# The sort's column sweep: loops written out, and VectorE making the scaled one-hots of three columns in five instead of two

## The reference

```python
def _gat_layer(x, src, dst, W, b, a, g, beta, N, concat):
    h = x @ W.T + b
    score = (h @ a[:d])[src] + (h @ a[d:])[dst]
    e = jnp.exp(-jax.nn.leaky_relu(score, ALPHA))
    h_prime = jax.ops.segment_sum(e[:, None] * h[dst], src, num_segments=N)
    ...                       # layer norm, elu
x = x + gnn(layernorm(x), ..., edge_index=[src, dst])   # 8 heads, then one output layer
x = x + moe(layernorm(x), ...)                          # 8 experts, the best 2
```

## Time and profile before

| what | value |
|---|---|
| median of three runs | 5569.01 us |
| profiled execution | 5574.75 us, of it 5573.0 us from its first to its last instruction |
| the sweep on VectorE | from 338.12 us (first L743) to 1096.45 us (last L738) |
| busy in the whole span | PE 84%, DVE 77%, POOL 73%, ACT 39% |
| mean granted clock of TensorE | 0.945 |

### The profile page before, as it was taken

One profiled execution on the slowest core, in us unless ns is written; L12 is line 12 of the kernel. 1 busy time (PEld: TensorE's weight loads), 2 busy tenths in 40 slices (PEclk: granted clock), 3 DMA queues, 4 the chain that ended last, 5 costly groups with the idle time before them and its releaser, 6 DMA issues. The chain is left out here.

```text
span 5573.0 us, 94092 instructions
## 1 busy us (share of the span) xinstructions
PE 4664.7 (84%) x20462; PEld 2641.7 (47%) x20462; DVE 4308.8 (77%) x15028; ACT 2185.1 (39%) x5836; POOL 4043.8 (73%) x4498
## 2 busy tenths in 40 slices
PE   7888888878888888888888866888788888888888
PEld 4532222333333333333333334666666666666666
DVE  6679999978888888888888866666666666666665
ACT  2258888723433344334333430222222222222223
POOL 2269999757777777777777757777777777777773
PEclk9999999989999999999999987999999999999999
DMA  3200000068888888888888865555555555554551
GB/s 76 66 17 1 0 0 0 1 191 246 242 243 242 243 243 243 244 243 243 242 243 242 242 184 158 137 137 140 137 138 140 137 139 138 137 140 136 139 141 53
DMA packets 331594, 847.59 MB, mean 152 GB/s; under 512 B 75165, under 2 KB 105167, under 8 KB 331187
## 3 DMA queue, kind: packets, MB, share of 16 engines
q0 software_dynamic: 219136, 683.92, 43.0%
q1 hardware_dynamic: 109763, 158.20, 9.7%
q10 hardware_dynamic: 2288, 0.79, 0.1%
HBM read 816.28 MB, written 26.36 MB: 151 GB/s over the span
## 5 line engine op out<-in xcount | busy, mean ns | idle before, releaser
L1382 POOL DMA_INDIRECT out_rows<-table,shared_node_of x1712 | 1641.8, 959 | 558.6 <-issue 479.5
L1137 POOL DMA_INDIRECT heads_rows<-table,shared_node_of x1712 | 1621.5, 947 | 575.0 <-issue 536.3
L1311 PE MATMUL heads_banks<-heads_rows,heads_hot 128*128 128x512 f32 x3424 | 1743.9, 631 | 140.1 <-DVE heads_rows L1193 136.0
L1527 PE MATMUL out_banks<-out_rows,out_hot 128*128 128x256 f32 x3424 | 1105.5, 416 | 121.9 <-DVE out_hot L1421 119.3
L1193 DVE TENSOR_TENSOR heads_rows<-heads_rows,heads_ps_k 128x512 f32<-128x512 f32 x1712 | 1163.0, 680 | 1.0
L1259 ACT ACTIVATE sums<-heads_banks x856 | 511.8, 598 | 1295.1 <-PE heads_banks L1311 1294.7
L1311 PEld LDWEIGHTS heads_banks<-heads_rows,heads_hot 128*128 128x128 f32 x3424 | 575.4, 193 | 674.8 <-DVE heads_rows L1193 327.4
L1527 PEld LDWEIGHTS out_banks<-out_rows,out_hot 128*128 128x128 f32 x3424 | 678.0, 206 | 311.5 <-DVE out_hot L1421 192.2
L582 POOL TENSOR_SCALAR sort_plain_lane<-sort_lanes_h,sort_place 125x128 f16<-125x128 f16 x990 | 688.8, 707 | 78.7 <-ACT sort_by_lane L893 62.7
L2064 PE MATMUL moe_ps_y<-late_w,moe_hidden 128*125 128x256 f32 x1600 | 536.6, 425 | 212.1 <-DVE moe_result L1957 153.7
L1487 ACT ACTIVATE out_weight<-out_score 128x4 f32<-128x4 f32 x428 | 87.8, 205 | 1415.8 <-DVE out_score L1416 1414.9
(11 more groups left out here) (347 smaller groups left out, 5847.6 us busy)
## 6 DMA issues: line engine op xcount, KB each, us to landing
heads_lanes<-lane_rows SPq DMA_DIRECT2D x214, 256.0 KB
out_lanes<-lane_rows SPq DMA_DIRECT2D x214, 256.0 KB
heads_rows<-table,shared_node_of POOLq DMA_INDIRECT x1712
out_rows<-table,shared_node_of POOLq DMA_INDIRECT x1712
table<-proj_rows SPq DMA_DIRECT2D x50, 227.5 KB
table<-mid_rows SPq DMA_DIRECT2D x50, 113.8 KB
sort_member<-in_x SPq DMA_DIRECT2D x5, 1120.0 KB
moe_x_raw<-in_x SPq DMA_DIRECT2D x50, 112.0 KB
```

The costliest lines, as they stand in the source:

```text
L1137: nc.gpsimd.indirect_dma_start(out=rows[:, g % RING, j, :], out_offset=None, in_=table[:, :], in_offset=bass.IndirectOffsetOnAxis(ap=node_ ...
L1311: ins = nc.tensor.matmul(banks[:, bass.ds(info[r], width)], hot[:, g % HOTS, j, :], rows[:, g % RING, j, 0:width], start=False, stop=True, ...
L1382: nc.gpsimd.indirect_dma_start(out=rows[:, g % RING, j, :], out_offset=None, in_=table[:, :], in_offset=bass.IndirectOffsetOnAxis(ap=node_ ...
L1527: ins = nc.tensor.matmul(banks[:, g % BANKS, j // RUN, :], hot[:, g % HOTS, j, :], rows[:, g % RING, j, 0:FEAT], start=j % RUN == 0, stop= ...
```

## The change

`SCALED` becomes (1, 3): slots 0, 2 and 4 are made by VectorE, so a turn has eleven VectorE instructions, six of them lane one-hots, and GpSimd and ScalarE make the lanes of two columns. The three hardware loops of VectorE, ScalarE and TensorE are written out column by column, with fixed places and fixed wait values; `hold` and its semaphore go, ScalarE's two waits stand directly ahead of the activation. The number of scaled columns ahead of column n is worked out by `scaled_before`.

```diff
-def hold(eng, sem, value, scratch):
-
-    eng.wait_ge(sem, value)
-    eng.sem_inc(scratch, 1)
...
-        SCALED = (1, 3, 4)
-        PER_TURN, SCALED_PART = COLUMNS // SLOTS * len(SCALED), PCOLS // SLOTS * len(SCALED)
+        SCALED = (1, 3)
         LANES_AHEAD = 5
+        def scaled_before(n):
+
+            return n // SLOTS * len(SCALED) + sum(at < n % SLOTS for at in SCALED)
...
-                for n in range(PCOLS):
+                for n in range(part * PCOLS, (part + 1) * PCOLS):
                     if n % SLOTS in SCALED:
+                        made = scaled_before(n)
                         if made >= LANES_AHEAD:
                             pool.wait_ge(s["scaled"], made - LANES_AHEAD + 1)
...
-                with dve.Fori(0, PCOLS // COLUMNS) as i:
-                    for j in range(COLUMNS):
-                        n = i * COLUMNS + j
-                        slot = j % SLOTS
-                        value_at = bass.ds(n + part * PCOLS, 1)
+                for n in range(part * PCOLS, (part + 1) * PCOLS):
+                    slot, value_at = n % SLOTS, slice(n, n + 1)
+
+                    dve.wait_ge(s["slot_used"], n + 1)
+                    if slot not in SCALED:
+                        nc.vector.tensor_scalar(by_lane[:, slot, 0, :], lanes_h[:, :], lane[:, value_at], low[:, value_at],
+                                                ALU.is_equal, ALU.mult)
+                        nc.vector.tensor_scalar(by_lane[:, slot, 1, :], lanes_h[:, :], lane[:, value_at], high[:, value_at],
+                                                ALU.is_equal, ALU.mult)
+                    nc.vector.tensor_scalar(by_tile[:, slot, :], count_tiles_h[:, :], tile[:, value_at], None, ALU.is_equal)\
+                        .then_inc(s["slot_made"], 1)
...
-                with act.Fori(first, last) as i:
-                    for j in range(COLUMNS):
-                        if j % SLOTS in SCALED:
-                            here, slot = SCALED.index(j % SLOTS), j % SLOTS
-                            n = j // SLOTS * len(SCALED) + here
-                            hold(act, s["lane_made"], i * PER_TURN + (part * SCALED_PART + n + 1), s["held_act"])
-                            hold(act, s["slot_used"], i * COLUMNS + (part * PCOLS + j + 1), s["held_act"])
+                for n in range(part * PCOLS + first * COLUMNS, part * PCOLS + last * COLUMNS):
+                    slot, value_at = n % SLOTS, slice(n, n + 1)
+                    if slot in SCALED:
+                        made = scaled_before(n)
+                        act.wait_ge(s["lane_made"], made + 1)
+                        act.wait_ge(s["slot_used"], n + 1)
...
-                with pe.Fori(first, last) as i:
+                for n in range(part * PCOLS + first * COLUMNS, part * PCOLS + last * COLUMNS):
+                    slot = n % SLOTS
+                    pe.wait_ge(s["slot_made"], n + 1)
+                    if slot in SCALED:
+                        pe.wait_ge(s["scaled"], scaled_before(n) + 1)
```

More of the change, by code:

```diff
@@ L511, in sort_edges @@
                  "numbered lane_made scaled slot_made slot_used swept packed_made packed_turned turn_out reach_made step_made "
-                 "step_known route_made route_used block_known row_ready laid_out dst_used cast held_act lane_known is_keyed is_spread is_compared picked "
+                 "step_known route_made route_used block_known row_ready laid_out dst_used cast lane_known is_keyed is_spread is_compared picked "
                  "local_made local_turned lane_kept lanes_stored")
@@ L577, in _ @@
                     pool.wait_ge(s["lane_known"], 1)
-                for n in range(PCOLS):
+                for n in range(part * PCOLS, (part + 1) * PCOLS):
                     if n % SLOTS in SCALED:
+                        made = scaled_before(n)
                         if made >= LANES_AHEAD:
                             pool.wait_ge(s["scaled"], made - LANES_AHEAD + 1)
-                        nc.gpsimd.tensor_scalar(plain_lane[:, made % LANES_AHEAD, :], lanes_h[:, :], lane[:, part * PCOLS + n:part * PCOLS + n + 1], None,
-                                                ALU.is_equal).then_inc(s["lane_made"], 1)
-                        made += 1
+                        nc.gpsimd.tensor_scalar(plain_lane[:, made % LANES_AHEAD, :], lanes_h[:, :], lane[:, n:n + 1], None, ALU.is_equal)\
+                            .then_inc(s["lane_made"], 1)
         @block.vector
@@ L882, in scale_columns @@
             def scale_columns(part, first, last):
-                with act.Fori(first, last) as i:
-                    for j in range(COLUMNS):
-                        if j % SLOTS in SCALED:
-                            here, slot = SCALED.index(j % SLOTS), j % SLOTS
-                            n = j // SLOTS * len(SCALED) + here
-                            hold(act, s["lane_made"], i * PER_TURN + (part * SCALED_PART + n + 1), s["held_act"])
-                            hold(act, s["slot_used"], i * COLUMNS + (part * PCOLS + j + 1), s["held_act"])
[L891 to L894, removed]
+                for n in range(part * PCOLS + first * COLUMNS, part * PCOLS + last * COLUMNS):
[4 more added lines that the diff above has]
+                        act.wait_ge(s["slot_used"], n + 1)
+                        nc.scalar.activation(by_lane[:, slot, 0, :], plain_lane[:, made % LANES_AHEAD, :], ACT.Copy, scale=low[:, value_at])
+                        nc.scalar.activation(by_lane[:, slot, 1, :], plain_lane[:, made % LANES_AHEAD, :], ACT.Copy,
+                                             scale=high[:, value_at]).then_inc(s["scaled"], 1)
             def take_sums(part):
@@ L995, in sweep_columns @@
             def sweep_columns(part, first, last):
-                with pe.Fori(first, last) as i:
[L998 to L1007, removed]
+                for n in range(part * PCOLS + first * COLUMNS, part * PCOLS + last * COLUMNS):
[3 more added lines that the diff above has]
+                        pe.wait_ge(s["scaled"], scaled_before(n) + 1)
+                    for number, ps in enumerate((ps_a, ps_b)):
+                        ins = nc.tensor.matmul(ps[:, part % 2, 0:PART_TILES], by_lane[:, slot, number, :], by_tile[:, slot, :],
+                                               start=False, stop=False)
+                    ins.then_inc(s["slot_used"], 1)
             def turn_sums(part):
```

10 lines of the change are left out of this document (removed).

## The result

The changed kernel takes 5686.99 us (median of four runs, 5683.77 to 5688.82), the kernel before 5568.78 us (median of four): a ratio of 1.0197, 95% interval 1.0172 to 1.0222, or +118 us. The prediction was 5690 us, in a range of 5660 to 5745.

What follows compares the result with a forecast made beforehand. VectorE was taken to bound the sweep: own work 812.8, borders 3.9, waits 8.8 and hold-up 53.4 give 878.9 us against 758.3, +120.6. On the median of 5569.01 that gave 5690 us, range 5660 to 5745.

Steps and rivals of the forecast that it cites:

- What bounds the sweep: In the sweep, VectorE sets the pace: busy 125.00 of 125 us, with the other engines' wait chains ending at it.
- Clean pitches, 0.223 and 0.225 us: VectorE in the sweep after GpSimd's last lane: 0.223 us per lane instruction, 0.225 per L757, start to start.
- Part one: Three columns in five on VectorE: 660 more lane instructions, +147.2 us; 330 fewer GpSimd lanes, -26.7 us of hold-up.
- part three: Start of the sweep: extra lane instructions lie in VectorE's wait for TensorE, so the start stays at 8.8 us.
- Part two: Sweep loops written out: ending the register work costed at nothing; bounds 0 to a few us, or a gain.
- The hold-up, 0.081 us per GpSimd lane: VectorE's remainder of 80.0 us in the sweep before, over 990 GpSimd lanes; 53.4 us for the new 660.
- the sum of 878.9 us: Forecast sweep on VectorE: own work 812.8, borders 3.9, waits 8.8, hold-up 53.4 us; against 758.3 before.
- The bounds of 0.05 and 0.16: Hold-up in us per GpSimd lane in common and long turns of the sweep; +100 to +173 us for the change.
- Lane instructions that become shorter when written out: Rival in the sweep: loop register work is the lane pitch, which falls toward 0.141 us; -42 us, 5527; chance 0.04.
- No hold-up: Rival in the sweep: GpSimd's hold-up of VectorE mostly goes; sweep 825.5 us, +67, 5636 us; chance 0.09.
- TensorE at half clock: Rival in the sweep: matmuls 0.31 us apart make TensorE the bound, 3.06 us per turn; +264, 5833 us; chance 0.03.
- GpSimd's lane as a full stop of VectorE: Rival in the sweep: each of 660 lanes stops VectorE some 0.6 us; +463, 6032 us; chance 0.02.

Runs made afterwards that it cites:

- e3_no_gpsimd: Changed kernel with SCALED empty, so VectorE makes the lanes of all five columns; +351 us against the kernel before, ratio 1.0554.
- e7_act_written: Kernel before with SCALED (1, 3) and ScalarE's loop alone written out; +124 us against the kernel before, ratio 1.0196.
- e2_ratio_only: Kernel before with SCALED (1, 3) alone, hardware loops kept; +145 us against the kernel before, ratio 1.0225.
- e10_by_tensor: e1_written_out with GpSimd waiting for TensorE's slot_used in place of ScalarE's scaled; -35 us against the kernel before, ratio 0.9929.
- e12_lane_later: Changed kernel with GpSimd also waiting for VectorE's tile of fifteen columns back; +149 us against the kernel before, ratio 1.0262.
- e1_written_out: Changed kernel with SCALED back at (1, 3, 4), loops still written out; -12 us against the kernel before, ratio 0.9979.
- e9_by_vector: e1_written_out with GpSimd also waiting for VectorE's tile ten columns back; +2 us against the kernel before, ratio 1.0001.
- e4_lanes_beside: e3_no_gpsimd plus 660 unused GpSimd lanes for slots 1 and 3; +388 us against the kernel before, ratio 1.0606.
- e8_block_of_three: Changed kernel with SCALED (2, 3, 4) in place of (1, 3); +51 us against the kernel before, ratio 1.0082.
- e11_memset_beside: e4_lanes_beside with GpSimd's unused comparisons replaced by memsets; +367 us against the kernel before, ratio 1.0650.

## Why the prediction was right, and where by luck

**What bounds the sweep**: right. VectorE was busy through it, and TensorE waited for its tiles; the sum of pitches alone gave the two sweeps without comparisons on GpSimd, 1114.0 and 1116.5 us, to 1.3 us. In the others the hold-up is what this sum leaves over, so they don't test it.

**Clean pitches, 0.223 and 0.225 us**: right to 1.2 us in 1114 (`e3_no_gpsimd`). They had been read from the last 3 us of the sweep, where GpSimd has ended, and not from the mean durations of 0.32 and 0.34.

**Part one, 660 more lane instructions, +147.2 us**: right. `e3_no_gpsimd` has 1320 more still, and its sweep is 1114.0 where the sum had 1120; most of the difference is in the waits at the start, 4.2 us and not 8.8. VectorE's longer head start takes 1.1 us off its first wait, and the second wait, 2.9 us in the kernel before, isn't there when no lane comes by way of ScalarE. In the changed kernel the two were 4.6 and 2.6, together 7.2: part three, which kept the start at 8.8, was 1.6 us off.

**Part two, the loops at nothing**: wrong in this term. The register work of VectorE is free, as the prediction had it (`e7_act_written`, 3 us in the time and none in the sweep), and so are its 66 jumps back, for which the prediction had left room for a gain. But "ScalarE and TensorE wait for VectorE anyway" looked only for their own time. ScalarE's delay moves GpSimd's lanes, and VectorE pays for where they start. At the new ratio the loop of ScalarE costs 31 us of sweep (905.9 against 874.5), at the old one the three loops together cost 13.0 (758.3 against 745.3); which of them, no run took apart.

**The hold-up, 0.081 us per GpSimd lane**: a good figure for the wrong reason. I took the mean over the turns of before as a price; it is no price but a place. The new ratio alone raises it to 0.122 (`e2_ratio_only`, +145 us, beyond the +120.6 of the sum but inside the +100 to +173), and the written-out loop brings it down to 0.074. Two errors nearly cancel: with the loops the hold-up was 80.3 us and not 53.4 (26.9 more), and writing them out took 31.5 off again (80.3 to 48.8). That they do is luck. What remains between the sum of 878.9 us and the measured 872.7 is 4.6 us of hold-up and 1.6 of waits. The bounds of 0.05 and 0.16 from the two kinds of turns held all kernels with a comparison on GpSimd, 0.053 to 0.124, and it is they, not the middle, that the argument had earned.

**The rivals.** Lane instructions that become shorter when written out: none. No hold-up: none, and of the kernels with comparisons on GpSimd none fell below 0.05 per lane. TensorE at half clock: the clock stayed at 1.00, also in `e3_no_gpsimd`. GpSimd's lane as a full stop of VectorE: no. By the Trainium skill, SBUF — State Buffer, section "Who interferes with whom", the one that issued second waits for the whole of the other, where VectorE runs in a 2-port perf mode (no run here shows the mode). Here a lane of 0.6 us held VectorE by 0.05 to 0.12 in the mean of a kernel and by 0.26 where it met two tile instructions, and a memset of 0.2 us held it by nothing, while memsets waited up to 32 us, far longer than any one instruction of VectorE. That the two engines hold each other, the page has right.

## What to carry to other kernels

Read the cost of an instruction in a full queue from start to start, in a stretch where nothing else runs, and count instructions; the durations here were longer than the pitches, up to about six times. When two engines hold each other up, the cost lies in where their instructions meet: any change to a third engine that shifts one of them, even one that saves only idle time, can move the bound, here by half a percent of the kernel. Look at both sides of a collision: an instruction that costs the busy engine nothing may itself wait for tens of microseconds. So don't carry a mean hold-up over to a changed pattern without its bounds, and try the wait that places the lane before the split of the work: it costs one line, but its effect has to be measured. Of the three waits tried here one gained (`e10_by_tensor`), one made the sweep 32 us longer than the changed kernel's (`e12_lane_later`) and one 13 us longer than `e1_written_out`'s (`e9_by_vector`).

## What the runs showed that I had not expected

- ScalarE's loop with held waits costs no ScalarE time that matters, yet 31 us of the sweep, through GpSimd's place.
- The hold-up of one GpSimd comparison ranges from 0.053 (`e4_lanes_beside`) to 0.124 us (`e8_block_of_three`) in the mean of a kernel, and the memset's is 0.002; but a memset of 0.2 us can last 32 us beside a busy VectorE (`e11_memset_beside`).
- In `e3_no_gpsimd` VectorE's records last 1.37 us with pitches of 0.22; the mean durations of the same instructions are 0.31 to 0.35 in the changed kernel. A duration in the trace is not the time that an instruction takes from its engine.
- The same 990 lanes and the same VectorE work give sweeps of 745 to 799 us, by the order of slots and by the semaphore that GpSimd waits for.
